# A perceiver block: the value projection of the attended context moves from the batch loop into the self-attention stage

## The chip, the core and the metric

The kernel runs on one core of a Trainium2 chip. A core has a tensor engine (PE, whose weight loads stand apart as PEld), a vector engine (DVE), a scalar engine (ACT), GpSimd (POOL) and a queue engine (SP) that here issues all transfers; each works its own instruction list in order, and they meet at semaphores. The metric is the device time of one execution in microseconds; lower is better.

## What is computed

One block of a perceiver for 16 batches of 64 latent rows with 256 channels, with a context of 1601 rows per batch:

```python
x = x + xattn(ctx_1024, layernorm(x), mask, ...)     # 16 heads of 64, keys and values from context and latents
x = x + attn(layernorm(x), W_q, ..., W_o, b_o)       # causal self-attention over 64 rows, 16 heads of 16
x = x + ffn(layernorm(x), w1, ..., wr, br)           # 4 experts of 1024, top 2 gates
```

In the cross-attention the key and value projections are absorbed. The queries have been multiplied by the key weights beforehand, scores are taken against the normalised context itself, and the softmax averages the context itself, not its values. What comes out of a batch is, for each of its 16 heads and 64 rows, an attended context of 256 channels. It must still go through the value weights of its head (256 to 64 channels) and then through the output weights (1024 to 256). Nothing lies between these two products but the gathering of the heads:

```python
out = einsum('bhln,bhnd->bhld', weight, v)            # v = context @ Wv, here applied after the average
out = out.transpose(0, 2, 1, 3).reshape(b, l, heads * dim_head) @ Wout
```

All products are in split precision: an operand is held as a high part (rounded) and a low part (the rest), and a product is three matmuls, high by high, high by low and low by high. So each operand costs a copy by ACT (high) and a subtraction by DVE (low).

## The kernel before

**Block 0** makes the absorbed queries. **Block 1** is the batch loop. A batch has two halves, X and Y, of 13 context chunks each; `plan_x` and `plan_y` write out by hand the order of events in them, and every engine walks the same list and does its own part of each event. The events are:

- K: transposes of the normalised context into keys; Q: the split of one pair of queries; A: a unit of scores, 6 matmuls with 416 columns into one of four banks, which DVE then adds to the bias (L926); E: exp of a pair of heads on ACT; P: DVE's scaling of that pair by the reciprocal of its sum (L938)
- T: transposes of four tiles of probabilities into one of two banks `t_bank` (L994), ACT's copy (L838) and DVE's subtraction (L902)
- V: 6 matmuls with 512 columns that add one chunk of the context to `o_bank` (L249, the helper `split_pair`, has the matmuls of all products)
- O: the high and low part of the attended context of half the heads (`outT`, L867 and L943)
- Y: the value projection. For four pairs of heads, PE multiplies the 128 columns of `wv` of the pair by the 128 columns (2 heads by 64 rows) of `outT`, 24 matmuls into a `t_bank`. Of each 128 x 128 result only the two 64 x 64 blocks on the diagonal are wanted; ACT and DVE copy these alone, in two instructions each on 64 partitions, into `ystage` (L826, L827, L897). SP stores `ystage` to DRAM as `y_scratch` (L747). ("Y", 0) stands at c = 1 of half X, ("Y", 1) at c = 2 of half Y, both for heads whose context was completed just before.
- N: the split of the context into values for V; S and H: moments and normalisation of the next batch's rows, with POOL's multiplications; W: the split of one sixteenth of the later stages' weights, in two events at c = 5 and c = 9 of half X: ACT copies each half (L832), and behind the second POOL subtracts the whole (L807), and SP stores it.

Half X of batch b does the second half of the heads' V of batch b - 1 beside its own first scores, so there are 15 full steps and a shorter one at either end. In each step SP's list is fixed too: weights, centre row, stores of `ystage`, row loads, queries and mask.

**Block 2** is the self-attention, in 8 row tiles of two batches each, as a software pipeline. `stages` runs s from -1 to 11, and in each s calls the steps in a fixed order, each for a tile with a lag; again all engines walk one list. a1 is the output projection of the cross-attention (24 matmuls with 256 columns, weights from `ysplit`, moving `wout`) and DVE's addition to x (L1292); a2n, a2 the normalisation (L1300) and its transposes (L1380); b1 the products for queries, keys and values; c1 scores and mask (L1320); c1m the maximum (L1325), its subtraction and exp; c2, c3 sums, transposes and averages; d1 to d3 the product with W_o, the residual and the next normalisation. `load_y` brings the projected rows of a tile, 1 MB, into a ring of two.

**Block 3** is the router and the experts, whose weights `w1` and `w2` of the first expert are loaded during block 2.

Of the kernel before, what the change touches and what calls it, by code (L numbers as in the profile page):

```python
# [27 lines left out]
P = 128  # L28
# [27 lines left out]
YRING = 2  # L56
# [11 lines left out]
X_AT = {"W": (5, 9), "P3": 10, "Y0": 1, "N0": 3, "N1": 7, "S4": 6, "S0": 10, "S1": 12}  # L68
Y_AT = {"P7": 9, "Y1": 2, "N2": 0, "N3": 0, "S2": 3, "S3": 3, "H": (3, 3, 5, 6, 8, 9, 10)}
# [3 lines left out]
def plan_x(has_a, has_b, has_next):  # L73
# [6 lines left out]
    for c in range(CH):  # L80
        if has_a:
# [9 lines left out]
            if c in X_AT["W"] and has_a:  # L91
                ev += [("W", X_AT["W"].index(c))]
            if c == X_AT["P3"] and has_b:
                ev += [("P", 3)]
            if c == 12 and has_b:
                ev += [("T", 0, 0)]
        if has_b:
# [3 lines left out]
            if c == X_AT["Y0"]:  # L101
                ev += [("Y", 0)]
# [11 lines left out]
def plan_y(has_prev, has_next):  # L114
# [9 lines left out]
    for c in range(CH):  # L124
# [6 lines left out]
        if c == Y_AT["Y1"] and has_prev:  # L131
            ev += [("Y", 1)]
# [25 lines left out]
def t_uses(ev):  # L158
    return [e for e in ev if e[0] in "YT"]
# [3 lines left out]
X_FIRST, X_MID, X_END = plan_x(True, False, True), plan_x(True, True, True), plan_x(False, True, False) + [("Y", 1)]  # L163
# [9 lines left out]
def load_y(sp, ysplit, y_scratch, rt, y_in):  # L173
    for q in range(2):
        sp.dma_start(ysplit[:, rt % YRING, q, :, :, :].bitcast(F32).rearrange("p a b l -> p a (b l)"),
                     y_scratch[q, :, :, 2 * rt:2 * rt + 2, :].rearrange("p a b l -> p a (b l)")
                     ).then_inc(y_in[rt % YRING], 16)

# [495 lines left out]
def block_1(nc, ins, F, y_scratch, w_scratch, shared, used, ctx):  # L674
# [21 lines left out]
    ystage, y_out, w_out = W["ystage"], W["y_out"], W["w_out"]  # L696
# [26 lines left out]
    out_done = sem("out_done")  # L723
# [7 lines left out]
    def _(sp):  # L731
# [11 lines left out]
        def store_y(b, h, e, index):  # L743

            sp.wait_ge(t_done, b.use(e) + 1)
            for q in range(2):
                sp.dma_start(y_scratch[q, :, 4 * h:4 * h + 4, index, :],  # L747
                             ystage[:, h, q, :, :].bitcast(F32)).then_inc(y_out[h], 16)
# [10 lines left out]
        def step(b, x, y):  # L759
            nxt = Batch(b.off + 1, b.turn)  # L760
            if ("W", 0) in x:
                load_w(b, b.lin(1, 0))
# [6 lines left out]
            if b.off == B:  # L769
# [4 lines left out]
                for h in range(2):  # L774
                    sp.wait_ge(y_out[h], 32 * 4)
                load_y(sp, W["ysplit"], y_scratch, 0, W["y_in"])
# [3 lines left out]
                load_y(sp, W["ysplit"], y_scratch, 1, W["y_in"])  # L780
# [13 lines left out]
            if ("W", 0) in x:  # L794
                store_w(b, b.lin(1, 0))
# [1040 lines left out]
```

## Time and profile before

| | |
|---|---|
| median of 3 runs | 2013.21 us (2013.17 to 2013.38) |
| the profiled execution | 2012.02 us, span 2009.3 us |
| PE busy | 1862.3 us, 93% of the span |
| DVE, ACT, POOL busy | 1366.7 (68%), 956.6 (48%), 601.1 us (30%) |
| moved by DMA | 146.88 MB, 73 GB/s over the span |

A profile has one execution. A line of its groups gives the source line, the engine and operation, the tiles out<-in with their shapes, the count, then the busy time, the mean of one in ns, the idle time of that engine just before them and what ended most of that. Matmuls are pipelined, so the time from one group's start to the next one's start is what it costs PE; the duration shown overlaps the next. The value 1.00 for PE's clock is 2.4 GHz and 0.50 is 1.2 GHz; a value between is a mean over a stretch. In the span, the batch loop runs to about 1651 us, block 2 from 1654.58 to about 1806, and the experts to the end.

### The profile page before, as it was taken

How to read it: one execution, taken by the hardware profiler on the slowest of the kernel's cores; microseconds unless marked ns; L12 is line 12 of the kernel's file. 1: busy time of each engine (PE TensorE's matmuls, PEld its weight loads, DVE VectorE, ACT ScalarE, POOL GpSimd, SP SyncE). 2: the span in 40 equal slices, each digit the busy share in tenths (PEclk: the TensorE clock that was granted, in tenths of full speed). 3: DMA queues.
4: the chain of work that ended last, by engine and by line, in shares of the span. 5: the costliest groups of instructions: out<-in, count | busy, mean ns of one | idle time of the engine just before them, and what ended most of it. 6: DMA issues, size and time to landing. Idle time of an engine off the chain costs nothing. (4 is left out here: it accounts for less than half of the span.)

```text
span 2009.3 us, 32957 instructions
## 1 busy us (share of the span) xinstructions
PE 1862.3 (93%) x10615; PEld 1622.6 (81%) x10615; DVE 1366.7 (68%) x3147; ACT 956.6 (48%) x1677; POOL 601.1 (30%) x647
## 2 busy tenths in 40 slices
PE   5889999999999999999999999999999987768998
PEld 4678888888888888888888888888888876656887
DVE  6576767676767777676767677767676635755656
ACT  4545455454545454545454545554545432225344
POOL 3433324241515151514141414242333004530000
PEclk9989999999999999999999999999999998969999
DMA  7821303121212120212121212122130056002221
GB/s 280 262 83 35 94 20 94 27 84 29 82 29 82 29 82 29 82 39 72 42 72 39 72 44 73 48 72 58 53 89 10 32 148 209 23 1 74 84 93 55
DMA packets 168939, 146.88 MB, mean 73 GB/s; under 512 B 104848, under 2 KB 144688, under 8 KB 168880
## 3 DMA queue, kind: packets, MB, share of 16 engines
q1 hardware_dynamic: 168880, 146.12, 24.2%
q8 instruction: 34, 0.56, 0.1%
q14 instruction: 25, 0.20, 0.0%
HBM read 97.85 MB, written 48.25 MB: 73 GB/s over the span
## 5 line engine op out<-in xcount | busy, mean ns | idle before, releaser
L249 PE MATMUL o_bank<-probT,val 128*128 128x512 f32 x2496 | 685.4, 410 | 16.9 <-DVE probT L902 14.3
L249 PE MATMUL s_bank<-late,qkT 128*128 128x416 f32 x3072 | 626.7, 354 | 10.9 <-DVE qkT L907 9.1
L249 PEld LDWEIGHTS s_bank<-late,qkT 128*128 128x128 f32 x3072 | 569.1, 188 | 39.9 <-issue 10.9
L249 PEld LDWEIGHTS o_bank<-probT,val 128*128 128x128 f32 x2496 | 438.7, 189 | 101.5 <-DVE probT L902 20.9
L860 ACT ACTIVATE prob<-prob,negmax 128x1665 f32<-128x1665 f32 x128 | 216.0, 1688 | 374.0 <-DVE negmax L931 374.0
L902 DVE TENSOR_TENSOR probT<-t_bank,probT 128x512 fp32r<-128x512 f32 x416 | 283.0, 687 | 152.2 <-ACT probT L838 148.1
L838 ACT ACTIVATE probT<-t_bank 128x512 fp32r<-128x512 f32 x416 | 242.7, 591 | 231.9 <-PE t_bank L994 230.2
L926 DVE CUSTOM_DVE_ANT_0 prob<-s_bank,bias 128x416 f32<-128x416 f32 x512 | 294.9, 585 | 47.0 <-PE s_bank L249 45.5
L994 PE MATMUL t_bank<-ident,prob 128*128 128x128 f32 x1664 | 251.8, 274 | 31.4 <-DVE prob L938 23.9
L994 PEld LDWEIGHTS t_bank<-ident,prob 128*128 128x128 f32 x1664 | 205.0, 141 | 76.5 <-issue 22.8
L807 POOL TENSOR_TENSOR late_y<-w_raw,late_y 128x1280 fp32r<-128x1280 f32 x16 | 46.8, 2923 | 631.9 <-ACT late_y L832 631.9
L938 DVE TENSOR_SCALAR prob<-prob,rsum 128x1665 f32<-128x1665 f32 x128 | 188.4, 1472 | 4.6
L907 DVE TENSOR_TENSOR qkT<-qk,qkT 128x256 fp32r<-128x256 f32 x128 | 58.9, 460 | 113.7 <-ACT qkT L844 113.7
L393 POOL TENSOR_TENSOR stage<-stage 128x1024 f32<-128x1024 f32 x48 | 126.1, 2627 | 28.5 <-ACT stage L338 28.5
L394 POOL TENSOR_TENSOR stage<-stage,g 128x1024 f32<-128x1024 f32 x48 | 124.8, 2600 | 3.8
L338 ACT ACTIVATE stage<-stage,shift,rstd 128x256 f32<-128x256 f32 x224 | 119.9, 592 | 1.6 <-POOL shift L375 1.2
L897 DVE TENSOR_TENSOR ystage<-t_bank,ystage 64x256 fp32r<-64x256 f32 x64 | 27.0, 422 | 103.3 <-ACT ystage L827 102.9
L249 PEld LDWEIGHTS t_bank<-outT,wv 128*128 128x128 f32 x768 | 91.7, 194 | 5.5 <-issue 2.7
L249 PE MATMUL hbank<-xn2T,ffn_w 128*128 128x512 f32 x384 | 90.7, 393 | 5.1 <-ACT stage L1562 5.1
L249 PE MATMUL t_bank<-outT,wv 128*128 128x128 f32 x768 | 90.6, 275 | 2.3 <-DVE outT L943 2.3
L249 PEld LDWEIGHTS hbank<-xn2T,ffn_w 128*128 128x128 f32 x384 | 71.2, 188 | 23.1 <-ACT stage L1562 8.5
L1562 ACT ACTIVATE stage<-hbank,ffn_b 128x512 f32<-128x512 f32 x64 | 43.9, 688 | 79.0 <-PE hbank L249 70.5
(198 smaller groups left out, 1975.7 us busy)
## 6 DMA issues: line engine op xcount, KB each, us to landing
stage<-in_ctx SPq DMA_DIRECT2D x48, 512.0 KB, 3.8
w_scratch<-late_y SPq DMA_DIRECT2D x16, 1280.0 KB, 6.3
qk<-qk_scratch SPq DMA_DIRECT2D x16, 1024.0 KB, 6.8
ffn_w<-w_scratch SPq DMA_DIRECT2D x16, 1024.0 KB, 7.4
w_raw<-in_wall SPq DMA_DIRECT2D x16, 640.0 KB, 6.9
qk_scratch<-qk_own SPq DMA_DIRECT2D x16, 512.0 KB, 3.9
qk_scratch<-wraw SPq DMA_DIRECT2D x16, 512.0 KB, 4.3
y_scratch<-ystage SPq DMA_DIRECT2D x64, 128.0 KB, 2.1
```

What stands on the lines that cost most here:

```text
L249: mm = pe.matmul(out, weights(a), moving(b), start=first and n == 0, stop=last and n == 2)
L338: act.activation(self.raw[s, c, :], self.raw[s, c, :], ACT.Identity, bias=self.shift[s, m:m + 1], scale=self.rstd[s, m:m + 1]).then_inc(se ...
L393: link(eng.tensor_tensor(rows, rows, raw[:, 13:14, :].to_broadcast([P, 4, D]), ALU.subtract))
L394: eng.tensor_tensor(rows, rows, g1[:, :].unsqueeze(1).to_broadcast([P, 4, D]), ALU.mult).then_inc(self.keys_done, 1)
L807: pool.tensor_tensor(w_split[:, 1, :], w_raw[:, :], w_split[:, 0, :].bitcast(F32), ALU.subtract).then_inc(w_low, 1)
L838: act.activation(probT[:, slot, 0, :], bank[:, :], ACT.Copy).then_inc(t_high, 1)
L860: act.activation(prob[:, i, :], prob[:, i, :], ACT.Exp, bias=negmax[:, i:i + 1], accum_out=psum_[:, i:i + 1]).then_inc(exp_done, 1)
L902: dve.tensor_tensor(probT[:, slot, 1, :], bank[:, :], probT[:, slot, 0, :].bitcast(F32), ALU.subtract).then_inc(t_done, 1)
L907: dve.tensor_tensor(qkT[:, i % 2, :, 1, :], qk32[:, i, :, :, :].rearrange("p k h l -> p k (h l)"), qkT[:, i % 2, :, 0, :].bitcast(F32), AL ...
L926: apart(dve.tensor_tensor_reduce(out=prob[:, i, s], in0=s_bank[j][:, 0:QTR], in1=W["bias"][:, s], scale=1.0, scalar=NEG, op0=ALU.add, op1= ...
L938: dve.tensor_scalar(prob[:, i, :], prob[:, i, :], rsum[:, i:i + 1], None, ALU.mult).then_inc(prob_done, 1)
L994: mm = pe.transpose(bank[:, t * P:(t + 1) * P], prob[:, 4 * h + t, c * P:(c + 1) * P], ident[:, :])
```

## The change

The event Y is gone from the loop. The attended context `outT` itself, high and low part, goes to DRAM, in two stores of 1 MB per batch (`store_o` to `o_scratch`), one for each half of the heads. ACT may write `outT` for one half when the store of the other half has landed. The event W is now one piece, at c = 6 of half X behind V. `wv` moves to the tiles that live through all blocks, and the order of SP's other work is kept.

Block 2 gets four steps y0 to y3 per row tile, two tiles ahead of a1's tile in the pipeline, so that s runs from -2. A unit is half of the heads for two batches, 2 MB, read from `o_scratch` into a ring of three, of which two places are those of the experts' `w1` and `w2`; these two are now loaded when the last units have been used. A piece is two pairs of heads: 12 matmuls with 256 columns into one bank, then ACT's and DVE's copies of the diagonal blocks, two instructions each, into `ysplit`, which has one buffer. a1 follows when all four pieces of its tile are there. The transposes of a2 share a bank with a1 now.

```diff
-X_AT = {"W": (5, 9), "P3": 10, "Y0": 1, "N0": 3, "N1": 7, "S4": 6, "S0": 10, "S1": 12}
-Y_AT = {"P7": 9, "Y1": 2, "N2": 0, "N3": 0, "S2": 3, "S3": 3, "H": (3, 3, 5, 6, 8, 9, 10)}
+X_AT = {"W": 6, "P3": 10, "N0": 3, "N1": 7, "S4": 6, "S0": 10, "S1": 12}
+Y_AT = {"P7": 9, "N2": 0, "N3": 0, "S2": 3, "S3": 3, "H": (3, 3, 5, 6, 8, 9, 10)}
...
-            if c in X_AT["W"] and has_a:
-                ev += [("W", X_AT["W"].index(c))]
...
             ev += [("V", 1, c)]
-            if c == X_AT["Y0"]:
-                ev += [("Y", 0)]
+            if c == X_AT["W"] and has_a:
+                ev += [("W",)]
...
+def load_o(sp, to, o_scratch, n, arrived):
+    rt, h = n // 2, n % 2
+    sp.dma_start(to.rearrange("p b k q n -> p b (k q n)").bitcast(F32),
+                 o_scratch[h, :, 2 * rt:2 * rt + 2, :]).then_inc(arrived, 16)
...
+        def store_o(b, h, index):
+
+            wait(sp, out_done[h], b, 2, 0)
+            sp.dma_start(o_scratch[h, :, index, :], outT[:, :, :, :].rearrange("p k q n -> p (k q n)").bitcast(F32)
+                         ).then_inc(o_out[h], 16)
...
             if has_next(y):
                 F.load_centre(sp, nxt, nxt.lin(1, 0))
 
                 wait(sp, val_done, nxt, 4, -3)
-            if ("Y", 0) in x:
-                store_y(b, 0, ("Y", 0), b.lin(1, -1))
+            if ("O", 1) in x:
+                store_o(b, 0, b.lin(1, -1))
             if has_next(y):
                 for g in range(4):
                     F.load_rows(sp, nxt, nxt.lin(1, 0), g)
-            if ("Y", 1) in x + y:
-                store_y(b, 1, ("Y", 1), b.lin(1, -1))
+            if ("O", 1) in x:
+                store_o(b, 1, b.lin(1, -1))
...
                     wait(act, pv_done, b, 26, 13 * (h + 1) - 26 * h)
                     wait(act, x0_done, b, 1, 1 - h)
+                    wait(act, o_out[1 - h], b, 16, 0)
...
-        for s in range(-1, RT + 4):
-            for name, lag in (("d3n", 4), ("a1", -1), ("d3", 4), ("c1", 2), ("d1", 3), ("b1", 1), ("c1m", 2),
-                              ("a2n", 0), ("b1v", 1), ("a2", 0), ("d2", 3), ("c2", 2), ("b2", 1), ("c3", 2)):
+        for s in range(-2, RT + 4):
+            for name, lag in (("d3n", 4), ("a1", -1), ("y0", -2), ("d3", 4), ("c1", 2), ("y1", -2), ("d1", 3), ("b1", 1),
+                              ("c1m", 2), ("a2n", 0), ("b1v", 1), ("y2", -2), ("a2", 0), ("d2", 3), ("c2", 2), ("y3", -2),
+                              ("b2", 1), ("c3", 2)):
...
+        load_o(sp, units[1], o_scratch, 1, o_in[1])
         load_split(sp, wv, w_scratch, WCOLS["wvs"][0], w_in[2])
+        load_o(sp, units[2], o_scratch, 2, o_in[2])
         load_split(sp, wo, w_scratch, WCOLS["wos"][0], w_in[3])
...
+        for n in range(ORING, 2 * RT):
+            if n == 2 * RT - 2:
                 for h in range(2):
...
+                    sp.wait_ge(W["o_out"][h], 16 * B)
+            sp.wait_ge(S["y_full"], 2 * (n - ORING) + 2)
+            load_o(sp, units[n % ORING], o_scratch, n, o_in[n % ORING])
...
+        sp.wait_ge(S["y_full"], 2 * (2 * RT - 2))
+        load_split(sp, E["w1"], w_scratch, W1_AT[0], W["w1_in"])
...
+            if name[0] == "y":
+                piece = int(name[1])
+                act.wait_ge(S["y_full"], 4 * t + piece + 1)
+                if t >= 1:
+                    act.wait_ge(S["x1_full"], t)
+                for u in range(2):
+                    rows = slice(u * L, u * L + L)
+                    copy = act.activation(ysplit[rows, 0, 2 * piece:2 * piece + 2, :, :].rearrange("p a b l -> p (a b) l"),
+                                          heads_of(bank[1])[rows, :, u, :], ACT.Copy)
+                copy.then_inc(S["y_high"], 1)
...
+            if name[0] == "y":
+                piece = int(name[1])
+                n = 2 * t + piece // 2
+                pe.wait_ge(o_in[n % ORING], 16 * (n // ORING + 1))
+                if 4 * t + piece > 0:
+                    pe.wait_ge(S["y_low"], 4 * t + piece)
+                for i in range(2):
+                    pair, a = 2 * piece + i, 2 * (piece % 2) + i
+                    for k in range(KD):
+                        mm = split_pair(pe, bank[1][:, i * 2 * P:(i + 1) * 2 * P],
+                                        lambda q: W["wv"][:, k, q, pair * P:(pair + 1) * P],
+                                        lambda q: units[n % ORING][:, :, k, q, a * P:(a + 1) * P], k == 0, k == KD - 1)
+                mm.then_inc(S["y_full"], 1)
...
```

## Rows read from the trace of the kernel before

**Rows 1.** The page, engine totals and one of the costliest groups.

```profile
PE 1862.3 (93%) x10615; PEld 1622.6 (81%) x10615; DVE 1366.7 (68%) x3147; ACT 956.6 (48%) x1677; POOL 601.1 (30%) x647
...
L994 PE MATMUL t_bank<-ident,prob 128*128 128x128 f32 x1664 | 251.8, 274 | 31.4 <-DVE prob L938 23.9
```

**Rows 2.** Windows: stretch, length, busy time per engine (instructions), PE clock, DMA share, GB/s.

```profile
900.00:1000.00 100.00, 96.98 (x547) 86.44 (x546) 71.45 (x174) 50.80 (x89) 33.63 (x36) 1.00 0.21 58
...
1750.00:1800.00 50.00, 34.89 (x346) 28.96 (x346) 32.49 (x62) 15.29 (x30) 20.03 (x25) 0.68 0.01 1
```

**Rows 3.** PE in the loop, in time: start, us, instructions, [idle before <-releaser].

```profile
891.56 0.63 PE L994 MATMUL t_bank<-ident,prob 128*128 128x128 f32 x4 [1.12 <-DVE prob L938]
...
907.44 2.79 PE L249 MATMUL t_bank<-outT,wv 128*128 128x128 f32 x24
910.07 2.48 PE L249 MATMUL s_bank<-late,qkT 128*128 128x416 f32 x12
...
985.55 1.67 PE L249 MATMUL o_bank<-probT,val 128*128 128x512 f32 x6 [0.96 <-DVE probT L902]
988.33 0.63 PE L994 MATMUL t_bank<-ident,prob 128*128 128x128 f32 x4 [1.12 <-DVE prob L938]
```

**Rows 4.** DVE in the same batch, in time.

```profile
911.07 0.86 DVE L897 TENSOR_TENSOR ystage<-t_bank,ystage 64x256 fp32r<-64x256 f32 x2 [2.78 <-ACT ystage L827]
...
976.82 1.09 DVE L938 TENSOR_SCALAR prob<-prob,rsum 128x1665 f32<-128x1665 f32 x1
...
985.60 2.59 DVE L938 TENSOR_SCALAR prob<-prob,rsum 128x1665 f32<-128x1665 f32 x1
```

**Rows 5.** ACT in the same batch, in time.

```profile
973.66 1.69 ACT L860 ACTIVATE prob<-prob,negmax 128x1665 f32<-128x1665 f32 x1 [2.79 <-DVE negmax L931]
...
983.57 0.72 ACT L832 ACTIVATE late_y<-w_raw 128x640 fp32r<-128x640 f32 x1
```

**Rows 6.** POOL in the same batch, in time.

```profile
984.38 2.93 POOL L807 TENSOR_TENSOR late_y<-w_raw,late_y 128x1280 fp32r<-128x1280 f32 x1 [39.58 <-ACT late_y L832]
```

**Rows 7.** A DMA issue group (KB each, median us to landing); a window of block 2.

```profile
ffn_w<-w_scratch SPq DMA_DIRECT2D x16, 1024.0 KB, 7.4
...
1672.00:1676.00 4.00, 1.52 (x12) 1.08 (x10) 2.50 (x4) 0.60 (x1) 3.77 (x5) 1.00 1.07 359
```

**Rows 8.** Timelines of DVE and PE at the end of the loop.

```profile
1645.70 1.41 DVE L943 SCALAR_TENSOR_TENSOR outT<-o_bank,x0T,outT 128x512 fp32r<-128x512 f32 x2 [3.60 <-ACT outT L867]
...
1654.58 5.00 PE L249 MATMUL bank<-late,late_y 128*128 128x256 f32 x24 [3.24 <-PEq L1769]
```

**Rows 9.** PE in one steady stage of block 2, in time.

```profile
1729.41 1.64 PE L249 MATMUL bank<-late,xnT 128*128 128x512 f32 x6
...
1735.55 0.44 PE L1380 MATMUL bank<-ident,stage 128*128 128x128 f32 x2 [3.06 <-DVE stage L1300]
...
1739.37 3.14 PE L249 MATMUL bank<-late,late_y 128*128 128x256 f32 x24
```

**Rows 10.** DVE in the same stage, in time.

```profile
1727.62 0.42 DVE L1292 TENSOR_TENSOR x<-bank,stage 128x256 f32<-128x256 f32 x1 [2.25 <-PE bank L249]
...
1731.70 1.21 DVE L1325 TENSOR_REDUCE mx<-sc 128x16 f32<-128x1024 f32 x1
...
1734.14 1.35 DVE L1300 TENSOR_SCALAR stage<-x,mv,rstd 128x256 f32<-128x256 f32 x1
...
1742.55 0.42 DVE L1292 TENSOR_TENSOR x<-bank,stage 128x256 f32<-128x256 f32 x1 [2.01 <-PE bank L249]
```

**Rows 11.** The tile ystage: count, ns min/median/max, first and last start.

```profile
L897 DVE TENSOR_TENSOR ystage<-t_bank,ystage x64: 416/422/430, 176.1 to 1652.6; 64x256 fp32r<-64x256 f32 x64
...
L827 ACT ACTIVATE ystage<-t_bank x32: 378/379/379, 175.7 to 1651.8; 64x256 fp32r<-64x256 f32 x32
```

**Rows 12.** Windows of 4 us in block 2, columns as in rows 2.

```profile
1732.00:1736.00 4.00, 0.94 (x9) 0.73 (x8) 3.96 (x4) 1.06 (x1) 3.84 (x3) 1.00 0.00 0
...
1796.00:1800.00 4.00, 2.27 (x32) 1.73 (x30) 1.12 (x3) 0.38 (x1) 0.00 (x0) 0.50 0.00 0
```

More of the change, by code:

```diff
@@ L55 @@
 HRING = 7
-YRING = 2
+ORING = 3
 S_BANK = (4, 5, 6, 3)
@@ L96, in plan_x @@
                 ev += [("T", 0, 0)]
+        if c == X_AT["W"] and has_a and not has_b:
+            ev += [("W",)]
         if has_b:
@@ L722, in block_1 @@
     out_high = sem("out_high")
-    out_done = sem("out_done")
+    out_done = [sem(f"out_done{h}") for h in range(2)]
     w_raw_in, w_high, w_low = sem("w_raw_in"), sem("w_high"), sem("w_low")
@@ L888, in half @@
                 kind = e[0]
[L889 removed]
+                if kind == "T":
                     dve.wait_ge(t_high, b.use(e) + 1)
                     bank = t_bank[b.bank(e)]
[L893 to L899 removed]
                 if kind == "T":
@@ L1206, in run @@
                     act.wait_ge(S["v_full"], t - 1)
-                act.activation(doubled(xnT[:, z, 0, :, :]), twice(bank[1][:, 0:D]), ACT.Copy
+                act.activation(doubled(xnT[:, z, 0, :, :]), twice(bank[0][:, D:2 * D]), ACT.Copy
                                ).then_inc(S["xnT_high"], 1)
@@ L1231, in run @@
                     act.wait_ge(S["o_full"], t - 1)
-                act.activation(attT[:, z, :, 0, :], bank[7][:, 0:D].rearrange("p (k x) -> p k x", k=KD), ACT.Copy
+                act.activation(attT[z][:, :, 0, :], bank[7][:, 0:D].rearrange("p (k x) -> p k x", k=KD), ACT.Copy
                                ).then_inc(S["attT_high"], 1)
@@ L1289, in run @@
             z = t % 2
+            if name[0] == "y":
+                piece = int(name[1])
+                dve.wait_ge(S["y_high"], 4 * t + piece + 1)
+                for u in range(2):
+                    rows = slice(u * L, u * L + L)
+                    high, rest = (ysplit[rows, q, 2 * piece:2 * piece + 2, :, :].rearrange("p a b l -> p (a b) l") for q in range(2))
+                    last = dve.tensor_tensor(rest, heads_of(bank[1])[rows, :, u, :], high.bitcast(F32), ALU.subtract)
+                last.then_inc(S["y_low"], 1)
             if name == "a1":
@@ L1303, in run @@
                 dve.wait_ge(S["xnT_high"], t + 1)
-                low(doubled(xnT[:, z, 1, :, :]), twice(bank[1][:, 0:D]), doubled(xnT[:, z, 0, :, :]), "xnT_low")
+                low(doubled(xnT[:, z, 1, :, :]), twice(bank[0][:, D:2 * D]), doubled(xnT[:, z, 0, :, :]), "xnT_low")
             if name == "b1":
@@ L1757, in _, with build @@
             give_back(t)
-def build(nc, ins, out, lat_scratch, qk_scratch, y_scratch, w_scratch, gate_scratch):
+def build(nc, ins, out, lat_scratch, qk_scratch, o_scratch, w_scratch, gate_scratch):
     with ExitStack() as ctx:
```

135 lines of the change are left out of this document (51 added, 84 removed).

## The prediction

> **What bounds the kernel now.** I read the page first: PE is busy for 93% of the span [rows 1]. The windows show that this holds in the batch loop and not behind it: from 900 to 1000 us PE is busy 97 of 100 us at full clock, from 1750 to 1800 it is busy 34.9 of 50 at a mean clock of 0.68 [rows 2]. So a microsecond of PE work is worth a microsecond in the loop, and in the self-attention stage it is worth what it adds to the chain between the engines. The PE timeline of the loop shows how little PE waits there. One batch is 988.33 - 891.56 = 96.77 us, and its larger waits are 0.96 and 1.12 us at the end of half X [rows 3]; the second returns in each batch, 23.9 us over the run [rows 1].
>
> **Removed from the loop: the projection.** One "Y" is 24 matmuls with 128 columns, from 907.44 to the next work at 910.07: 2.63 us, 110 ns each [rows 3]. A batch has two. DVE had idled 2.78 us before it took Y's result [rows 4], so it was done with all that PE needs next: the score units and transposes behind Y can move up by the whole 2.63 us. I count full value, 31 x 2.63 = 81.5 us (the 32nd is in the tail below). ACT and DVE lose the copies of Y too, 2 x 2 x 0.42 = 1.7 us of DVE per batch [rows 11], so they don't take PE's place as the bound.
>
> **Moved in the loop: the weight split "W".** It was two halves at c = 5 and 9 of half X and becomes one piece at c = 6. This is a second gain. At c = 9 ACT ran the second half at 983.57 [rows 5], between exp and the copy of probT for which PE then waited 0.96 us [rows 3]. Its end released POOL's subtraction at 984.38 for 2.93 us [rows 6], and DVE's scaling of prob beside it took 2.59 us, where one with POOL idle took 1.09 [rows 4]; PE waited 1.12 us for that scaling. With W gone from here the copy comes 0.6 us sooner, PE's group of 985.55 starts at 984.9 and is through at 986.4, and DVE's scaling starts at 984.95 and is done at 986.05. So the transposes of 988.33 start at 986.4: 1.9 us less per batch, times 15 is 28 us. At the new place ACT was free for 2.79 us before 973.66 [rows 5], enough for a piece of twice 0.72 us, and POOL runs from about 972.4 to 975.3, ahead of the scaling at 976.82 [rows 4]. Bounds: at best both waits whole, 15 x 2.08 = 31 us; at worst POOL meets another scaling and 1.5 us per batch are lost, -22 us. I take 28, because the gap of 1.5 us between POOL and the next scaling can be read off.
>
> The stretched scaling is what the Trainium skill describes (SBUF — State Buffer, in the part on its ports): a VectorE operation in a two-port mode and a GpSimd operation exclude each other for a whole instruction. What it makes of this place is the 1.5 us that the rows show.
>
> **Added in the loop: stores and waits.** A batch stores two pieces of 1 MB in place of four of 128 KB; DMA's share is 0.21 here [rows 2]. The store of half 0 stands on SP's queue ahead of the next row loads and holds them up by less than the 7.4 us that 1 MB takes from issue to landing [rows 7]; those rows are read some 25 us later. ACT's new wait, for the other half's store, has the copy of o_bank and PE's next group behind it, and comes some 20 us after that store was issued. Cost nothing; with that cover gone, up to 5 us per batch.
>
> **The tail of the loop.** DVE had subtracted the last context by 1647.11; then came the last Y and its stores, and the next stage's first matmul at 1654.58 [rows 8]. Now only a store is issued in between, about 1.2 us: 6 us gained. The loop gives 81.5 + 28 + 6 = **115 us**.
>
> **Added behind the loop: the projection for two batches at once.** There are 8 row tiles with 4 pieces each, and a piece is 12 matmuls with 256 columns. The output projection has 24 of these in 3.14 us, 0.16 of it the end of the pipeline (2.79 against 2.63 us at Y) [rows 3, 9]: 1.49 us per piece, 6.0 per tile, 48 in all. ACT needs 2 x 0.38 and DVE 2 x 0.42 us per piece [rows 11], 3.0 and 3.4 us per tile. There is one PSUM bank, and each piece waits for the subtraction of the one before: 1.64 + 0.77 + 0.86 and three handovers of 0.05 are 3.4 us in series, 13.6 per tile, with the output projection's 3.1 behind it.
> A steady stage now takes 1742.55 - 1727.62 = 14.9 us [rows 10]. I lay the new order over it, from DVE's start behind the output projection. Piece 0: PE 1.5, ACT 2.35, DVE 3.25. DVE masks scores until 4.95; piece 1, which PE starts at 3.3, is ready at 5.8 and done at 6.65. Its PE part stands ahead of the query product (1.64 us, [rows 9]), so DVE's bias starts at 7.05, and max, subtraction and normalisation, 1731.70 to 1735.49 today, 4.1 us after the stage's start [rows 10], run from 7.7 to 11.45. Piece 2 uses PE's hole of 3.06 us [rows 9] but is subtracted only at 12.95, behind the mask of values; piece 3 starts on PE at 13.4 and its DVE part, behind the row sums, ends at 16.85. The output projection starts there and ends at 20.0. **So a stage takes 20 us in place of 15**; DVE works 15.8 of the 20.
> The seven intervals between output projections took 1742.55 - 1659.6 = 83 us [rows 8, 10]. Now: 16.7 and 17.5 while little else runs, 18.5, 19.5 and 3 x 20, which is 132: +49. Ahead of them comes a stage of four pieces alone. At half clock the 24 matmuls took 5.0 us [rows 8], so a piece takes 4.4 us and that stage 17.6: +18. If one of the next two intervals runs at half clock too, +6. **Sum: +73 us.** Bounds: 11 + 49 = +60 at full clock throughout, +122 at half clock throughout (below).
>
> **Loads.** 16 units of 2 MB are read in place of 1 MB per tile, 31 MB after the first. In this stage loads reached 359 GB/s [rows 7], so a unit takes 6 to 7 us and is wanted every 10, with three in flight. Only units 1 and 2 are close: unit 1 lands some 8.5 us after the start and is wanted at 8.8. The expert weights come after the last unit and more than 50 us before their use. Nothing counted; the price of slow loads is a rival.
> A rule of the Trainium skill speaks against the change (DMA: Bandwidth & Descriptors, in Latency and other measured facts): row pitches in HBM at large powers of two slow a copy, to 207 GB/s at 512 KiB, and o_scratch has 128 KiB per partition. At that figure, an estimate from the page, a unit takes 10 us and two of them as long as a stage.
>
> **The sum.** The profiled execution took 2012.0 us (span 2009.3), 1.2 us under the median. 2013.2 - 115 + 73 = **1971 us**.
>
> **The rivals.**
> *Half clock behind the loop* (ends slower). The clock falls where PE waits often [rows 2, 12], and each new piece makes PE wait. At half clock the same layout gives 27.7 us per steady stage (output projection +2, the two early pieces +1.05 each, query product +1.1, late transposes, last product and piece 3 +2.5), 184 us for the seven intervals, so +101, +18 ahead of them and +3 behind: +122, and 2013.2 - 115 + 122 = 2020. It decides once the stage grows by over 115 us. Against it: from 1732 to 1736 PE was busy 0.94 of 4 us and the clock stayed 1.00; the new stage has PE busy 17 of 20. For it: 0.50 at 1796 with PE busy 2.27 of 4 [rows 12]. The Trainium skill (TensorE: Matmul & The Clock Gate, HAM oscillation) has this case, bursts broken by waits that fall back to half rate. Chance 0.10.
> *W's move gives nothing*, because POOL meets another scaling: 2013.2 - 87 + 73 = 1999. For it: POOL's start hangs on ACT's queue, which shifts. Chance 0.15.
> *The stage becomes bound by loads.* At 200 GB/s, above the 1 MB in 7.4 us of [rows 7], 15 units take 157 us and the intervals follow: some 20 us more, 1991. Against it the 359 GB/s. Chance 0.12.
> *Own case*, 1971, own range 1955 to 1985: 0.60. Left over, slower than all: 0.03.
>
> **How the numbers follow.** The range takes in W's and the loads' case: 1950 to 2005 leaves out the clock case and the leftover, 0.13, and tails. Under 0.2% (4 us) this kernel's runs can't tell a change. Slower by more: 0.10, most of the clock case and the leftover; same: 0.03; faster: 0.87.
>
> **What would show it.** Batches of 89.6 us (96.77 - 5.26 - 1.9); no wait for prob ahead of the transposes at the end of half X, and a scaling of 1.09 us there; output projections 20 us apart in the steady part, with PE's clock near 1.0; the stage longer by 73 us. It is wrong if PE's waits in the loop grow once Y is gone, if PE waits for loads in the stage, or if the clock stays at 0.50.

## The result, and the profile after

| | before | after |
|---|---|---|
| median of the runs, us | 2013.3 | 1954.2 (1951.2 to 1956.9, 4 runs) |
| profiled execution, us | 2012.0 | 1955.6 |
| its span, us | 2009.3 | 1953.8 |
| ratio | | 0.9703, 95% interval 0.9686 to 0.9721 |

The change takes 59 us away. The forecast was 1971, the range 1950 to 2005: the sign and the mechanism held, and the kernel is 17 us better than the forecast. The kernel before was run again beside the experiments: its medians were 2012.0 to 2014.3 us, its single runs 2006.7 to 2016.4, a wider spread than the 4 us that the prediction took as the least that can be told. So a difference of a few us between the totals of two kernels shows little, and the stages of the profiles have to be compared.

The page of after: the totals of the engines (busy us, share, instructions), then two of the costliest groups (busy, mean ns of one, idle before and its releaser).

```profile
PE 1816.8 (93%) x10231; PEld 1579.8 (81%) x10231; DVE 1344.6 (69%) x3147; ACT 952.7 (49%) x1661; POOL 602.7 (31%) x647
...
L965 PE MATMUL t_bank<-ident,prob 128*128 128x128 f32 x1664 | 250.4, 273 | 11.3 <-DVE probT L884 7.3
...
L920 DVE TENSOR_SCALAR prob<-prob,rsum 128x1665 f32<-128x1665 f32 x128 | 166.0, 1297 | 4.6
```

PE has 384 matmuls fewer and is as full as it was, 93% [rows 1]. The transposes' wait for the scaling of prob, 23.9 us in rows 1, is no longer the largest part of that group's idle time, which fell from 31.4 to 11.3 us.

The windows of after in the stretch of rows 2, and one in the steady part of block 2 (columns as in rows 2).

```profile
900.00:1000.00 100.00, 98.72 (x539) 87.80 (x538) 73.77 (x185) 52.97 (x90) 34.09 (x35) 1.00 0.27 87
...
1616.00:1690.00 74.00, 62.58 (x651) 58.41 (x652) 51.55 (x105) 26.80 (x61) 28.65 (x36) 0.93 0.47 171
```

In the loop PE is now busy 98.7 us of 100, so almost nothing but PE's own work is left there. In the steady part of block 2 its mean clock is 0.93.

One batch of after, PE in time (columns as in rows 3): the same point of two batches in the first and the last line, the larger waits between.

```profile
883.17 1.39 PE L246 MATMUL s_bank<-late,qkT 128*128 128x416 f32 x6 [0.48 <-DVE qkT L889]
...
922.00 1.67 PE L246 MATMUL o_bank<-probT,val 128*128 128x512 f32 x6 [0.33 <-DVE probT L884]
...
960.97 0.66 PE L965 MATMUL t_bank<-ident,prob 128*128 128x128 f32 x4 [0.35 <-DVE probT L884]
...
972.59 1.40 PE L246 MATMUL s_bank<-late,qkT 128*128 128x416 f32 x6 [0.47 <-DVE qkT L889]
```

A batch takes 972.59 - 883.17 = 89.42 us; 89.6 was forecast. The wait of 0.96 for probT is now 0.33, and the one of 1.12 for prob is gone. The next fence, ACT, POOL and DVE of after in the same batch, shows why: the weight split, and then the two scalings of prob that follow it.

```profile
907.77 1.27 ACT L820 ACTIVATE late_y<-w_raw 128x1280 fp32r<-128x1280 f32 x1
...
909.12 2.96 POOL L802 TENSOR_TENSOR late_y<-w_raw,late_y 128x1280 fp32r<-128x1280 f32 x1 [24.59 <-ACT late_y L820]
...
913.90 1.09 DVE L920 TENSOR_SCALAR prob<-prob,rsum 128x1665 f32<-128x1665 f32 x1
...
922.05 1.09 DVE L920 TENSOR_SCALAR prob<-prob,rsum 128x1665 f32<-128x1665 f32 x1
```

POOL's subtraction ends at 912.08, 1.8 us ahead of the scaling at 913.90, and the scaling of 922.05, which answers to that of 985.60 in rows 4, takes 1.09 us in place of 2.59.

Of block 2, first PE at its start (columns as in rows 3).

```profile
1533.20 1.67 PE L246 MATMUL bank<-late_y,wv 128*128 128x256 f32 x12 [3.00 <-PEq L1784]
1536.80 1.67 PE L246 MATMUL bank<-late_y,wv 128*128 128x256 f32 x12 [1.94 <-DVE ysplit L1287]
1542.25 2.93 PE L246 MATMUL bank<-ffn_w,wv 128*128 128x256 f32 x12 [3.78 <-DMA ffn_w<-o_scratch]
1547.02 1.66 PE L246 MATMUL bank<-ffn_w,wv 128*128 128x256 f32 x12 [1.84 <-DVE ysplit L1287]
1550.52 3.09 PE L246 MATMUL bank<-late,ysplit 128*128 128x256 f32 x24 [1.84 <-DVE ysplit L1287]
```

Then PE in one steady stage. The lines with 12 matmuls whose weights are `wv` (not `wv_self`) are the pieces of the projection.

```profile
1625.20 1.58 PE L246 MATMUL bank<-ffn_w,wv 128*128 128x256 f32 x12
...
1628.63 1.66 PE L246 MATMUL bank<-ffn_w,wv 128*128 128x256 f32 x12 [1.22 <-DVE ysplit L1287]
...
1633.18 1.58 PE L246 MATMUL bank<-ffn_w,wv 128*128 128x256 f32 x12
1636.83 0.44 PE L1395 MATMUL bank<-ident,stage 128*128 128x128 f32 x2 [2.06 <-DVE stage L1299]
...
1639.32 2.54 PE L246 MATMUL bank<-ffn_w,wv 128*128 128x256 f32 x12
...
1643.65 3.07 PE L246 MATMUL bank<-late,ysplit 128*128 128x256 f32 x24 [0.30 <-issue]
```

And DVE's additions behind the output projections, which answer to the first and last line of rows 10.

```profile
1553.65 0.42 DVE L1291 TENSOR_TENSOR x<-bank,stage 128x256 f32<-128x256 f32 x1 [3.27 <-PE bank L246]
1570.49 0.42 DVE L1291 TENSOR_TENSOR x<-bank,stage 128x256 f32<-128x256 f32 x1 [3.26 <-PE bank L246]
1587.36 0.42 DVE L1291 TENSOR_TENSOR x<-bank,stage 128x256 f32<-128x256 f32 x1 [3.26 <-PE bank L246]
...
1625.40 0.42 DVE L1291 TENSOR_TENSOR x<-bank,stage 128x256 f32<-128x256 f32 x1 [2.67 <-PE bank L246]
1646.76 0.42 DVE L1291 TENSOR_TENSOR x<-bank,stage 128x256 f32<-128x256 f32 x1 [2.43 <-PE bank L246]
...
1688.01 0.42 DVE L1291 TENSOR_TENSOR x<-bank,stage 128x256 f32<-128x256 f32 x1 [2.45 <-PE bank L246]
```

The seven intervals are 16.8, 16.9, 17.6, 20.5, 21.4, 21.5 and 19.8 us, 134.4 in all. In the stage that begins with the addition at T = 1625.40, the normalisation is through, and PE's transposes start, at T + 11.43 us (forecast 11.45). The last piece took 2.54 us in place of 1.6, and the output projection started at T + 18.25 (forecast 16.9).

**Where the 55.5 us of span went.** The mark between the two halves is the first matmul of block 2, the second one the router's first product behind the last attention tile (1808.39 us before, 1752.46 after).

| | before | after | difference | forecast |
|---|---|---|---|---|
| to the first matmul of block 2 | 1654.58 | 1533.20 | -121.4 | -115 |
| from there to the router | 153.8 | 219.3 | +65.5 | +73 |
| the rest | | | +0.4 | 0 |

### The profile page after: what moved, and what is told of

It reads as the page before. It is cut to its first block and busy times, and to the rows that moved or that the text cites. A ratio compares the mean times of both kernels' runs of the same rounds, so it can differ in the third digit from the quotient of the medians.

```text
span 1953.8 us, 31948 instructions
## 1 busy us (share of the span) xinstructions
PE 1816.8 (93%) x10231; PEld 1579.8 (81%) x10231; DVE 1344.6 (69%) x3147; ACT 952.7 (49%) x1661; POOL 602.7 (31%) x647
## 5 line engine op out<-in xcount | busy, mean ns | idle before, releaser
L246 PEld LDWEIGHTS o_bank<-probT,val 128*128 128x128 f32 x2496 | 438.7, 189 | 90.1 <-DVE probT L884 11.6
L965 PE MATMUL t_bank<-ident,prob 128*128 128x128 f32 x1664 | 250.4, 273 | 11.3 <-DVE probT L884 7.3
L920 DVE TENSOR_SCALAR prob<-prob,rsum 128x1665 f32<-128x1665 f32 x128 | 166.0, 1297 | 4.6
L896 DVE TENSOR_TENSOR late<-s_bank,late 128x512 fp32r<-128x512 f32 (+1 forms) x128 | 69.5, 584 | 36.6 <-ACT late L844 36.6
L361 POOL TENSOR_TENSOR small<-stats 128x9 f32<-128x9 f32 (+1 forms) x32 | 6.8, 212 | 245.5 <-DVE stats L327 245.5
L327 DVE BATCH_NORM_STATS2 stats<-stage 128x6 f32<-128x256 f32 x224 | 78.7, 412 | 0.0
```

The costliest lines, as they stand in the source:

```text
L246: mm = pe.matmul(out, weights(a), moving(b), start=first and n == 0, stop=last and n == 2)
L327: dve.bn_stats(self.stats[:, STAT[c], :], self.raw[:, c, :]).then_inc(self.stat_done, 1)
L896: dve.tensor_tensor(keyT[:, k, 1, a * P:z * P], bank[:, at:at + (z - a) * P], keyT[:, k, 0, a * P:z * P].bitcast(F32), ALU.subtract).then_ ...
L920: dve.tensor_scalar(prob[:, i, :], prob[:, i, :], rsum[:, i:i + 1], None, ALU.mult).then_inc(prob_done, 1)
L965: mm = pe.transpose(bank[:, t * P:(t + 1) * P], prob[:, 4 * h + t, c * P:(c + 1) * P], ident[:, :])
```

## The experiments

Two theories stood for each half. For the loop, that the two parts of the change pay separately, Y's matmuls with their whole duration and W's move with 1.9 us per batch because of two waits; the rival was that one of them only opens room for the other, or that W's move gives nothing. For block 2, that the single PSUM bank and DVE's chain set the intervals; the rivals were loads and the clock. The "time to block 2" below is the start of its first matmul, and the length of block 2 runs from there to the router's.

**W's move alone, on the kernel before.**

```diff
-X_AT = {"W": (5, 9), "P3": 10, ...
+X_AT = {"W": 6, "P3": 10, ...
...
-                    act.activation(w_split[:, 0, s], w_raw[:, s], ACT.Copy).then_inc(w_high, 1)
+                    act.activation(w_split[:, 0, :], w_raw[:, :], ACT.Copy).then_inc(w_high, 1)
```

> The kernel before, with the weight split W alone changed: one piece at c = 6 of half X instead of halves at c = 5 and 9. The projection Y stays in the loop. My theory (W's two events made both waits at the end of half X): a batch takes 96.77 - 1.9 = 94.9 us, the scaling of prob there takes 1.09 instead of 2.59 us, and the whole is 28 to 31 us faster: 1982 to 1985 us. Rival (the waits went away only because Y was gone): within 3 us of the kernel before.

Measured: 1974.8 us, ratio 0.9818 (0.9794 to 0.9841). PE (first line) and DVE of this run at the place of rows 3 and 4:

```profile
965.82 1.67 PE L251 MATMUL o_bank<-probT,val 128*128 128x512 f32 x6 [0.33 <-DVE probT L903]
```

```profile
965.87 1.09 DVE L939 TENSOR_SCALAR prob<-prob,rsum 128x1665 f32<-128x1665 f32 x1
```

Both waits changed as the prediction had said, and a batch takes 94.7 us, 2.1 less. Block 2 starts at 1620.39, 34.2 us earlier. The total fell by more than that, 39.4 us against the 2014.3 that the kernel before took beside it; block 2 took 148.8 us here against 153.8 in the profile of before, with nothing changed in it. So W's move is worth some 34 us, and the last 5 are in a stage that the edit doesn't touch. That is also more than 15 batches of 2.1 us. Most of the rest, 3 us, comes from the first, short step, where PE waits for a scaling of prob before its first transposes of probabilities. Before, then this run:

```profile
118.56 1.75 PE L994 MATMUL t_bank<-ident,prob 128*128 128x128 f32 x7 [7.14 <-DVE prob L938]
```

```profile
116.44 1.13 PE L995 MATMUL t_bank<-ident,prob 128*128 128x128 f32 x8 [4.02 <-DVE prob L939]
```

That wait is 7.1 to 7.2 us in the three profiles with W at c = 5 and 9, and 4.0 to 4.1 in the seven with W at 6.

**The change with W back at its old places.** The same edit backwards, on the kernel after.

> The changed kernel with W back as two halves at c = 5 and 9. My theory: the loop loses 1.9 to 2.1 us per batch, period 91.5 us, the two waits of 0.96 and 1.12 us are back, 1954 + 28 to 31 = 1982 to 1985 us. Rival (removal of Y also cured the waits): 1954 us.

Measured: 1991.3 us, 0.9883 (0.9863 to 0.9903). PE, DVE and POOL of this run at the end of half X:

```profile
940.19 1.68 PE L244 MATMUL o_bank<-probT,val 128*128 128x512 f32 x6 [0.96 <-DVE probT L883]
...
942.96 0.63 PE L964 MATMUL t_bank<-ident,prob 128*128 128x128 f32 x4 [1.10 <-DVE prob L919]
```

```profile
940.24 2.58 DVE L919 TENSOR_SCALAR prob<-prob,rsum 128x1665 f32<-128x1665 f32 x1
```

```profile
939.01 2.92 POOL L800 TENSOR_TENSOR late_y<-w_raw,late_y 128x1280 fp32r<-128x1280 f32 x1 [36.93 <-ACT late_y L819]
```

With W at its old place the waits of 0.96 and 1.10 us are those of rows 3 again, although Y is gone from the loop. Four loops can now be compared by the start of block 2:

| | Y in the loop | Y out |
|---|---|---|
| W at 5 and 9 | 1654.58 | 1565.03 |
| W at 6 | 1620.39 | 1533.20 |

W's move is worth 34.2 and 31.8 us, Y's 89.6 and 87.2: they nearly add, and neither opens room for the other. In total times W's move brings 39.4 us on the one side and 37.1 on the other, and Y's own move only 21 to 23, since what it saves in the loop is mostly spent in block 2. The run missed its expectation by 6 us, and block 2 holds this: it took 226.0 us, 6.7 more than in after, with the same code. One interval between output projections, 16.8 us in after, was 21.5 here:

```profile
1587.00:1608.00 21.00, 13.68 (x72) 12.80 (x71) 4.06 (x11) 3.03 (x8) 0.74 (x2) 0.67 0.70 275
```

PE's mean clock is 0.67 in that window. So total times of this kernel vary by some us with the clock in block 2, and what an edit does to the loop is better read from the start of block 2.

**POOL's subtraction held back, on the kernel before.** W stays at c = 5 and 9, but POOL starts only when DVE has scaled the fourth pair. This takes away the meeting and leaves ACT's order.

```diff
...
                 wait(pool, w_high, b, 2, 2)
+                if b.off > 0:
+                    wait(pool, prob_done, b, 8, 4)
                 pool.tensor_tensor(w_split[:, 1, :], w_raw[:, :], ...
```

> The kernel before with one wait more: POOL's subtraction for W waits until DVE has scaled the fourth pair (P3), so that both no longer run side by side; W's two ACT copies stay where they are. My theory (an exclusive port is what stretches the scaling): scaling 1.09 us there, the wait of 1.12 us for prob gone, that of 0.96 us for probT still there; 1.28 us less per batch, 15 x 1.28 = 19 us, about 1994 us. Rival (the scaling is long for another cause): 2013 us. Rival 2 (POOL is then late for the next batch's normalisation): above 2013 us.

Measured: 1991.9 us, 0.9898 (0.9879 to 0.9917). PE, then DVE:

```profile
975.29 1.68 PE L249 MATMUL o_bank<-probT,val 128*128 128x512 f32 x6 [0.96 <-DVE probT L904]
```

```profile
975.34 1.09 DVE L940 TENSOR_SCALAR prob<-prob,rsum 128x1665 f32<-128x1665 f32 x1
```

The scaling is back at 1.09 us and the wait for it is gone; the 0.96 us wait for probT, which comes from ACT's order, stays. A batch is 95.36 us, 1.4 less where 1.28 was expected. So of W's 2.0 to 2.1 us, 1.4 are the meeting of POOL and DVE and some 0.6 are ACT's half piece in front of the copy. Block 2 starts at 1633.13, 21.5 us earlier, which is 15 times 1.43. One added wait in the old order would have brought a third of what the whole change did.

**Stores doubled.** Each store of the attended context is issued twice, to two places.

```diff
+            sp.dma_start(o_scratch[2 + h, :, index, :], outT[:, :, :, :].rearrange("p k q n -> p (k q n)").bitcast(F32)
+                         ).then_inc(o_out[h], 16)
...
-                    wait(act, o_out[1 - h], b, 16, 0)
+                    wait(act, o_out[1 - h], b, 32, 0)
```

> The changed kernel with each store of the attended context issued twice, the second to a spare part of DRAM, and all waits for the stores counting both. My theory (stores and ACT's wait for them are hidden): 1954 us, within 2 us, batch 89.4 us. Rival (stores delay row loads or the copy of o_bank): 1 to 5 us per batch, 1970 to 2030 us.

Measured: 1956.7 us, 0.9714 (0.9696 to 0.9732). The batch takes 89.38 us and block 2 starts at 1532.93, both as in after. A second set of stores costs the loop nothing, so the first set is hidden too.

**No loads in block 2.** All tiles read the unit that is there first.

```diff
-        load_o(sp, units[1], o_scratch, 1, o_in[1])
...
-        load_o(sp, units[2], o_scratch, 2, o_in[2])
...
-            load_o(sp, units[n % ORING], o_scratch, n, o_in[n % ORING])
...
-                pe.wait_ge(o_in[n % ORING], 16 * (n // ORING + 1))
+                pe.wait_ge(o_in[0], 16)
...
-                                        lambda q: units[n % ORING][...]
+                                        lambda q: units[0][...]
```

> The changed kernel without the loads of units 1 to 15 of the attended context in the self-attention stage; all pieces multiply unit 0. This leaves the context of all but two batches out of the result. My theory (the stage is bound by the chain of pieces, loads are hidden but for the wait for unit 1 of 3.8 us): 3 to 5 us less, 1949 to 1951 us, intervals between output projections still 17 to 21 us. Rival (bound by loads): 20 us less or more, 1934 us.

Measured: 1950.6 us, 0.9689 (0.9666 to 0.9712): with 31 MB less to read the median is 3.7 us lower, and the 95% intervals of the two ratios overlap, so it is not shown that anything was gained. The seven intervals between output projections are 16.8, 16.8, 17.6, 20.5, 21.4, 19.8 and 21.4, the same within 0.1 us but for one 21.4 that changed places. Even at the one wait for a load, ahead of the third piece of the first tile, nothing was gained. In the two profiles the difference lies elsewhere: block 2 starts 0.7 us earlier, and behind the intervals, where no unit is loaded, it is 2.2 us shorter. PE in the first tile of this run:

```profile
1532.47 2.90 PE L246 MATMUL bank<-late_y,wv 128*128 128x256 f32 x12 [2.99 <-PEq L1781]
1537.31 2.90 PE L246 MATMUL bank<-late_y,wv 128*128 128x256 f32 x12 [1.94 <-DVE ysplit L1284]
1542.05 2.90 PE L246 MATMUL bank<-late_y,wv 128*128 128x256 f32 x12 [1.84 <-DVE ysplit L1284]
1546.79 1.67 PE L246 MATMUL bank<-late_y,wv 128*128 128x256 f32 x12 [1.84 <-DVE ysplit L1284]
```

Three pieces ran at 2.90 us, the lower of the clock's two levels, and the first addition came 20.99 us behind the first piece, where after had 20.45. The wait was gone and the clock cost as much. This is one pair of profiles, and the clock at this point may differ from run to run.

**Two banks in the first four tiles.** The odd pieces go to bank 5, which nothing else uses that early; a piece then waits for the subtraction of the last but one.

```diff
+    def ybank(t, piece):
+        return bank[5 if t < TWO and piece % 2 else 1]
...
-                                          heads_of(bank[1])[rows, :, u, :], ACT.Copy)
+                                          heads_of(ybank(t, piece))[rows, :, u, :], ACT.Copy)
...
-                if 4 * t + piece > 0:
-                    pe.wait_ge(S["y_low"], 4 * t + piece)
+                if 4 * t + piece > 1:
+                    pe.wait_ge(S["y_low"], max(4 * t + piece - (1 if 0 < t < TWO or t < TWO and piece else 0), 0))
...
```

> The changed kernel with a second PSUM bank for the odd pieces of the first four row tiles (bank 5, which nothing else uses until the third stage with scores). A piece then waits for the subtraction of the piece before the last. My theory (the serial chain through one bank, 3.4 us per piece, sets the first intervals): they fall from 16.8 to the 12.6 to 14 us that two units of 2 MB take to load, some 3 x 3.3 us less, 1944 us, and PE now waits for loads there. Rival (loads are the bound already): 1954 us. Rival (a lower clock, since PE waits for DMA): 1954 or more.

Measured: 1939.3 us, 0.9641 (0.9618 to 0.9664), 15 us under after where 10 were expected. The first three intervals went from 16.8, 16.9 and 17.6 to 12.7, 13.1 and 13.9, 11.6 us less: one bank had set them. Another 2.1 us of the 15 lie ahead of block 2, which starts at 1531.07 here, and have nothing to do with the edit. What is late next shows on PE:

```profile
1540.20 4.48 PE L246 MATMUL bank<-ffn_w,wv 128*128 128x256 f32 x24 [6.03 <-DMA ffn_w<-o_scratch]
...
1554.37 3.11 PE L246 MATMUL bank<-late_y,wv 128*128 128x256 f32 x24 [0.44 <-DMA late_y<-o_scratch]
```

The first wait for a load grew from 3.78 to 6.03 us, and a second one of 0.44 is new: with the bank out of the way the loads are the next thing near.

**Two banks everywhere, and piece 3 earlier.** In the last four tiles piece 2 goes to bank 5, and piece 3 stands directly behind it on PE, ahead of the transposes a2; c3, which uses bank 5 later in the stage, waits for the subtraction of the next piece.

```diff
-                              ("c1m", 2), ("a2n", 0), ("b1v", 1), ("y2", -2), ("a2", 0), ("d2", 3), ("c2", 2), ("y3", -2),
+                              ("c1m", 2), ("a2n", 0), ("b1v", 1), ("y2", -2), ("y3", -2), ("a2", 0), ("d2", 3), ("c2", 2),
...
+        return bank[5 if piece == (2 if t >= TWO else 1) or t < TWO and piece == 3 else 1]
...
+                if t + 4 < RT:
+                    pe.wait_ge(S["y_low"], 4 * (t + 4) + 3)
...
```

> The two-bank kernel of the run before, and for the last four row tiles too a second bank: piece 2 goes to bank 5 (free between the scores and the averages of a stage), and piece 3 stands directly behind piece 2, ahead of the transposes of the next tile. My theory (in the steady part the chain of pieces through one bank sets the interval of 21.4 us; piece 3 now fits into PE's hole ahead of the transposes): steady intervals 18.4 to 19 us, four of them, 10 us less: 1929 us. Rival (DVE's work, 15.8 us per stage, and its order set the interval): 1936 to 1939 us.

Measured: 1931.6 us, 0.9603 (0.9590 to 0.9617), faster than both kernels. The steady intervals are 18.3 and three times 18.5 us, 18.4 to 19 were expected. PE in one of these stages:

```profile
1617.88 3.01 PE L246 MATMUL bank<-ffn_w,wv 128*128 128x256 f32 x24
1621.54 0.44 PE L1400 MATMUL bank<-ident,stage 128*128 128x128 f32 x2 [0.65 <-DVE stage L1304]
```

PE does pieces 2 and 3 in one go where it had idled, the hole ahead of a2 is 0.65 us in place of 2.06, and no later matmul of the stage waits for a bank of the projection. The edit changes three things at once, the bank, the place of piece 3 and the hole, and the clock was 1.00 in this part. The next run shows that 1.6 of the 2.9 us between 21.4 and 18.5 are the clock's; the other 1.3 us belong to bank and order together, which no run parts.

**Useless matmuls in the hole.** To part the clock from the bank, 12 matmuls whose result is overwritten fill PE's hole ahead of a2 in the tiles from the third on. The bank and the order stay those of after.

```diff
...
+                if t >= 2:
+                    pe.wait_ge(w_in[3], 32)
+                    for n in range(12):
+                        pe.matmul(bank[0][:, D:2 * D], wo[:, 0, 0, 0:P], wo[:, 1, 0, :], start=n == 0, stop=n == 11)
+                pe.wait_ge(S["xn_done"], t + 1)
...
```

> The changed kernel with 12 matmuls of no use per row tile from the third on, in PE's hole of 2 us ahead of the transposes of the normalised rows (their result is overwritten). Theory (in the steady stage PE's clock falls for some us after that hole, which makes late pieces and products slow and the interval 21.4 in place of 19.8 us): clock near 1.00 there, the steady intervals 19.8 us, 4 to 6 us less in all, 1949 us. Rival (the clock has no part in the interval, or the filler delays the transposes): 1954 us or more.

Measured: 1946.7 us, 0.9681 (0.9668 to 0.9694): more work on PE, and 7.5 us less than after. The two intervals overlap by a little (after's begins at 0.9686), so the profile has to decide. PE in a steady stage and the window of after shown above:

```profile
1651.56 1.59 PE L1396 MATMUL bank<-wo_self 128*128 128x256 f32 x12
...
1653.81 0.44 PE L1399 MATMUL bank<-ident,stage 128*128 128x128 f32 x2 [0.65 <-DVE stage L1299]
...
1655.58 1.69 PE L246 MATMUL bank<-ffn_w,wv 128*128 128x256 f32 x12
```

```profile
1616.00:1690.00 74.00, 65.22 (x707) 60.79 (x708) 55.40 (x109) 26.50 (x60) 30.89 (x37) 1.00 0.46 171
```

The clock is 1.00 in place of 0.93, the last piece takes 1.69 us in place of 2.54, and the last four intervals, 20.5, 21.4, 21.5 and 19.8 in after, are 19.3 and three times 19.8. So the stage is 19.8 us long by its chain, and 1.6 us were the clock's. After itself has one interval of 19.8, behind a hole of 2.04 us: the clock need not fall at such a hole, but with the hole filled it fell in none of the four. Block 2 is 210.9 us long against 219.3, of which 4.5 us are these intervals and 4.3 the part behind them, where the matmuls stand in PE's holes too.

## Why the prediction was right, and where its sizes were off

**Y out of the loop: right.** Forecast 5.26 us per batch, whole value. On average over 14 batches and with W at its old places, a batch went from 96.79 to 91.44 us (5.35 less); with W moved it went from 94.73 to 89.40 (5.32 less). The ground given, that DVE had been idle 2.78 us before Y's result [rows 4], carried: nothing else took the freed time.

**W's move: right in both of its waits, a little small.** Forecast 1.9 us per batch and 28 in all; the runs give 2.1 and 2.0 per batch, 34.2 and 31.8 by the start of block 2. The two causes are shown apart: 1.4 us for POOL beside DVE, the rest for ACT. Per batch the term was 0.1 to 0.2 us too small, 2 to 3 us in all. The larger miss is a reading of rows 1. The prediction took the 23.9 us for a wait that returns in each batch; 15 times 1.12 are only 16.8, and the other 7.1 are the one wait in the short first step. W's move shortened that wait by 3.1 us and the step by 3.4 to 3.6 us, and the prediction counted nothing there.

**Ends of the loop: mis-sized.** The tail from one and the same batch's event to block 2 went from 81.8 to 69.7 us, 12.0 shorter, where the prediction's terms for it come to 2 x 2.63 + 6 = 11.3. Of the last part of it, from the last subtraction to block 2, 7.5 us became 0.8, 6.6 gained where 6 was forecast. The head, up to the second subtraction of an attended context, is 6.0 us shorter (217.79 to 211.81). One Y and one W, between the first such subtraction and the second, are 4.8 of it. The other 1.2 are the 3.4 us of W in the short first step less 2.2 us by which the scores of that step started later (90.37 before, 92.53 after); the eight profiles of the experiments have that start between 90.4 and 91.4, so most of the 2.2 us is this run's own. In sum: 14 batches by 7.38 are 103.4, with 12.0 and 6.0 the 121.4 us; forecast 115.

**Stores and ACT's wait at nothing: right**, shown by the doubled stores.

**The stage of pieces alone: its length right by luck, its term too large.** The prediction took the half clock for the whole first stage, 4.4 us per piece and 17.6 us. From the first piece to the first output projection it took 1550.52 - 1533.20 = 17.3 us, but made up of other parts. At full clock a piece takes 3.5 us in series (1547.02 to 1550.52; forecast 3.4), four take 14.0; one piece at the lower clock adds 1.3 us, and unit 1 adds 1.9 us. Of the 3.78 us of idle time that the profile puts down to the load, 1.84 us would have gone to the subtraction anyway; the piece could have started 7.1 us behind the first and started at 9.0, where the prediction had the unit landing at 8.5 and wanted at 8.8. So PE did wait for a load here, one of the signs by which the prediction wanted to be wrong, but for 1.9 us and once. What failed is the term beside it: +18 left the output projection as it was in rows 8, 5.00 us, and now it came behind busy time and took 3.09. From the start of block 2 to the first addition it is 20.45 us in place of 5.1, +15.3. Without loads three pieces ran at the lower clock, 4.7 to 4.8 us each, and the stage took 17.8 us, nearly as long.

**Seven intervals.** Forecast +49, and +6 for one interval at half clock; measured 134.4 - 82.8 = +51.6. The layout was good to 0.02 us at the normalisation (T + 11.43 against 11.45), and the early intervals 16.8, 16.9, 17.6 stand against 16.7, 17.5, 18.5. "Clock near 1.0" in the steady part was wrong: PE's 2 us hole ahead of a2 returns in each stage, and in three of the four the clock fell behind it for a part of the next pieces, 1.2 to 1.7 us per stage. The 20 us of the forecast are the 19.8 of a stage at full clock, which the filler run shows; there all seven intervals are 129.9 us, where the layout said 132. The interval at half clock did not come in after; in the run with W back one did in part, at 4.7 us. So it is luck that +49 and +6 together come near +51.6: the layout was 2 us too long, the clock took 4.5 us where it was put at nothing, and the +6 stood for an interval that did not come.

**Behind the intervals**, 1.4 us were gained (65.8 to 64.5) that the prediction had at nothing. The record has a measure for it: the same code took 65.8 us in before and 62.7 in the run with W's move alone, at a mean clock of 0.70 and 0.76. So 1.4 us are less than this part varies by from run to run.

**Loads at nothing: right in the sum.** The rule on row pitches of the Trainium skill (DMA: Bandwidth & Descriptors, in Latency and other measured facts) did not come true at this kernel's pitch of 128 KiB: the loads ran at 403 GB/s in the window below, and without any loads the seven intervals stayed as they were. That is no contradiction to its rows, which begin at 512 KiB.

```profile
1536.00:1544.00 8.00, 3.42 (x20) 3.25 (x21) 1.49 (x4) 0.76 (x2) 0.00 (x0) 0.89 1.02 403
```

**The rivals.** W's move giving nothing is refuted by two runs (34 and 32 us). The loads' case is refuted by the run without them, though the two-bank kernel shows them next in line. Half clock behind the loop came true only in small: 0.93 in the steady part, not 0.50, and 1.6 us per stage, not 7.7. The cause that the text had named, waits between bursts, is borne out by the filler run. The Trainium skill's case (TensorE: Matmul & The Clock Gate, HAM oscillation) is of that kind, bursts broken by waits that fall back to half rate, and the trace agrees in a milder form.

**The sum.** -121.4 + 65.5 + 0.4 = -55.5 of span, where -42 was forecast: 6.4 us of the miss are the loop's (3.4 in the full batches, 1.2 in the short first step, 0.7 in the tail, the rest rounding), and 7.5 block 2's (2.7 in the stage of pieces alone, 3.4 in the intervals, 1.4 behind them). The profiled executions differ by 56.4, and the medians by 59.1, since the profile of before lies 1.3 us under its median and that of after 1.4 over its own.

**What stays open.** Why the clock falls behind one hole and not behind the next, and in one run's early intervals and not in another's: block 2 of the kernel before took 153.8 us in one profile and 148.8 in another with the same code. How much of the last kernel's steady gain is the second bank and how much the new order is not shown either.

## What to carry to other kernels

Work that leaves a loop which one engine fills pays its whole duration there, but it must be costed again where it lands: here 24 matmuls in the batch were 2.6 us of PE, and in a stage of dependent steps they became a chain of 3.5 us per piece on one PSUM bank, so some 88 us saved became 21 to 23. Give moved work a second bank and a place in the engine's hole at once; that was worth another 23 us here, the clock's share included.

A diff may carry a second change that its name doesn't tell, and the first and last steps of a loop have to be looked at by themselves. Here the small move of a weight split, away from where POOL's subtraction met DVE's scaling, brought more of the gain than the projection's move, and it can be had without that move.

Read the effect of an edit at the end of the stage that it touches; a stage with holes on PE makes the total vary by several us with the clock.

## What the runs showed of the hardware that was not expected

A hole of 2.06 us on PE once in a stage of some 20 us went with a mean clock of 0.93; with 12 useless matmuls (1.59 us) in it, which left 0.65 us of hole, the clock was 1.00 and the stage 1.6 us shorter. The slow stretch is seen behind the hole, in the piece of 2.54 us that starts 2.5 us later. One of the four holes of after, 2.04 us, had no slow stretch behind it.

Where POOL and DVE meet, it is the one that came second that is longer. POOL and DVE of after at another place of the batch, where no W is:

```profile
946.60 2.40 POOL L390 TENSOR_TENSOR stage<-stage 128x1024 f32<-128x1024 f32 x1 [0.33 <-ACT stage L335]
949.08 3.08 POOL L391 TENSOR_TENSOR stage<-stage,g 128x1024 f32<-128x1024 f32 x1
956.65 2.39 POOL L390 TENSOR_TENSOR stage<-stage 128x1024 f32<-128x1024 f32 x1
```

```profile
947.03 2.85 DVE L920 TENSOR_SCALAR prob<-prob,rsum 128x1665 f32<-128x1665 f32 x1
```

POOL was first at 946.60 and took its 2.40 us; DVE, 0.43 us behind it, took 2.85 in place of 1.09 and ended 0.9 us after POOL. POOL's next operation, which started while DVE was still at it, took 3.08 where others took 2.39. In the short first step it is the other way round: DVE's scaling started first, at 104.99, and took its 1.09 us, and POOL, 0.16 us behind it, took 3.76 us where it takes 2.96 in a full batch.

```profile
105.15 3.76 POOL L802 TENSOR_TENSOR late_y<-w_raw,late_y 128x1280 fp32r<-128x1280 f32 x1 [27.74 <-ACT late_y L820]
```

So one such meeting, that of 947.03, is left in each batch of after. It costs PE nothing that its timeline shows, which marks no wait from 923 to 960 us, so moving it away promises little; no run tried it. The Trainium skill has it so (SBUF — State Buffer, in the part on its ports): whichever of the two starts first holds the ports for its whole instruction. The trace agrees, with the numbers above.
